# A Mixture-of-Experts kernel on one core: when SyncE asks for the weights of the next experts, and in which order

## What is computed

```python
dispatch = dispatch.at[flat_e, pos_c].add(tokens[tidx] * valid[:, None])   # 64 experts x 256 slots
g = jnp.einsum('ech,ehi->eci', dispatch, gate_w)      # gate_w, up_w: 64 x 512 x 256
u = jnp.einsum('ech,ehi->eci', dispatch, up_w)
expert_out = jnp.einsum('eci,eih->ech', jax.nn.silu(g) * u, down_w)   # down_w: 64 x 256 x 512
gathered = expert_out[flat_e, pos_c]
contrib = gathered * (topk_w.reshape(-1) * valid)[:, None]
output = jnp.zeros((t, h), tokens.dtype).at[tidx].add(contrib)
```

## Time and profile before

| | us |
|---|---|
| median of three runs | 1291.22 |
| their range | 1290.9 to 1291.5 |
| the profiled execution, as timed | 1295.88 |
| its span, first to last instruction | 1294.1 |
| PE busy | 1269.8 (98%) |
| DVE busy | 930.5 (72%) |
| ACT busy | 648.2 (50%) |
| POOL busy | 421.5 (33%) |
| HBM read and written | 178.18 MB and 71.39 MB |

### The profile page before, as it was taken

The page is one execution under the profiler, slowest core; times in us unless marked ns, Lnnn a source line. Parts: engine busy times, 40 slices in busy tenths (PEclk is TensorE's granted clock), DMA queues, the critical chain, the costliest instruction groups (busy, mean ns, idle before and its releaser), DMA issues.

```text
span 1294.1 us, 23005 instructions
## 1 busy us (share of the span) xinstructions
PE 1269.8 (98%) x7577; PEld 1118.6 (86%) x7577; DVE 930.5 (72%) x1853; ACT 648.2 (50%) x1130; POOL 421.5 (33%) x344
## 2 busy tenths in 40 slices
PE   8999999999999999999999999999999999999993
PEld 7888888888888888888889999999999999999993
DVE  7887787867878678785655777777777777777771
ACT  6422223222232223322255777777777777777771
POOL 1000000000000000000013666666666667677753
PEclk9999999999999999999999999999999999999997
DMA  8246654575545755446447999999999999999995
GB/s 309 85 137 153 135 132 113 143 168 115 133 111 145 168 107 137 112 116 136 137 132 211 297 288 302 290 299 293 298 289 297 293 293 284 299 290 301 286 250 66
DMA packets 204777, 263.66 MB, mean 204 GB/s; under 512 B 41012, under 2 KB 131016, under 8 KB 204744
## 3 DMA queue, kind: packets, MB, share of 16 engines
q1 hardware_dynamic: 175272, 191.40, 51.5%
q0 software_dynamic: 28672, 71.32, 24.5%
q10 hardware_dynamic: 800, 0.53, 0.2%
HBM read 178.18 MB, written 71.39 MB: 193 GB/s over the span
## 4 chain that ended last, share of the span: by engine, by line
PE 91%; POOL 3%; issue 3%; DVE 1%; DMA 1%; ACT 0%; POOLq 0%; ACTq 0%
PE pmm L1344 17%; PE pmm L1343 17%; PE pmm L1342 16%; PE pout L1342 11%; PE pout L1344 11%; PE pout L1343 11%; PE ptr L1599 4%; PE plp L1407 2%; POOL out_dram L1758 2%; POOL xbuf L1748 1%; PE pmm L1617 1%; PE ptr L1354 1%; DMA out_dram<-xbuf,slot_cols 1%; PE plp L1436 1%; PE plp L1416 1%
## 5 line engine op out<-in xcount | busy, mean ns | idle before, releaser
L1344 PE MATMUL pmm<-xt_hi,proj_lo 128*128 128x256 f32 (+1 forms) x768 | 241.2, 314 | 0.0
L1343 PE MATMUL pmm<-xt_lo,proj_hi 128*128 128x256 f32 (+1 forms) x768 | 241.1, 314 | 0.0
L1344 PE MATMUL pmm<-xt_hi,sgu_lo 128*128 128x256 f32 (+1 forms) x764 | 240.1, 314 | 0.0
L1343 PE MATMUL pmm<-xt_lo,sgu_hi 128*128 128x256 f32 (+1 forms) x764 | 240.1, 314 | 0.0
L1342 PE MATMUL pmm<-xt_hi,proj_hi 128*128 128x256 f32 (+1 forms) x736 | 232.5, 316 | 0.0
L1342 PE MATMUL pmm<-xt_hi,sgu_hi 128*128 128x256 f32 (+1 forms) x732 | 231.3, 316 | 0.0
L1742 POOL TENSOR_TENSOR earlier<-earlier,chosen 128x64 bf16<-128x64 bf16 x64 | 24.2, 378 | 611.4 <-DVE chosen L976 607.7
L1748 POOL DMA_INDIRECT xbuf<-rows,slot_cols x128 | 165.6, 1294 | 85.7 <-issue 37.4
L569 ACT ACTIVATE feat<-pmm,ab 128x512 f32<-128x512 f32 x66 | 45.4, 689 | 286.4 <-PE pmm L1344 286.4
L1343 PEld LDWEIGHTS pmm<-xt_lo,proj_hi 128*128 128x128 f32 x768 | 144.2, 188 | 11.2
L1343 PEld LDWEIGHTS pmm<-xt_lo,sgu_hi 128*128 128x128 f32 x764 | 143.4, 188 | 11.2
(11 more groups left out here) (220 smaller groups left out, 2640.1 us busy)
## 6 DMA issues: line engine op xcount, KB each, us to landing
raw<-in_L_ffn_gate_w_dram SPq DMA_DIRECT2D x64, 512.0 KB
raw<-in_L_ffn_up_w_dram SPq DMA_DIRECT2D x64, 512.0 KB
raw<-in_L_ffn_down_w_dram SPq DMA_DIRECT2D x64, 512.0 KB
outs<-in_L_attn_x_dram SPq DMA_DIRECT2D x32, 512.0 KB, 3.7
out_dram<-outs SPq DMA_DIRECT2D x32, 512.0 KB, 3.1
xbuf<-in_L_attn_x_dram SPq DMA_DIRECT2D x52, 256.0 KB, 8.1
raw<-xn SPq DMA_DIRECT2D x52, 256.0 KB, 6.5
rows<-raw SPq DMA_DIRECT2D x39, 256.0 KB, 4.8
```

The costliest lines, as they stand in the source:

```text
L1343: pe.matmul(psum, lh, rl, start=False, stop=False)
L1344: ins = pe.matmul(psum, ll, rh, start=False, stop=final and n == len(pairs) - 1)
```

## The change

Only SyncE's stream in the experts' part changes. Its unit becomes `refill(n)`: wait until `e_turned` says that TensorE has turned the rows of expert n-2, request gate of n, request down of n-2, request up of n. Each request keeps the wait on its own buffer. Gate and up of expert 3 stay outside, as do the two downs at the end. The first pass of the loop is written out, since expert 4 to 7's waits need constants.

```diff
-            def refill_gate_up(e):
-
-                for m, source in enumerate((gate_w, up_w)):
-                    sp.wait_ge(egu_hi_made[m], e.n - 1)
-                    sp.wait_ge(egu_lo_made[m], e.n - 1)
-                    load_half(e.b, m, source[e.n])
+            def refill_half(e, m, source):
+
+                sp.wait_ge(egu_hi_made[m], e.n - 1)
+                sp.wait_ge(egu_lo_made[m], e.n - 1)
+                load_half(e.b, m, source[e.n])
...
-            refill_gate_up(turn(3))
-            refill_down(turn(2))
-            with sp.Fori(0, CHUNKS - 3) as m:
+            def refill(e):
+
+                sp.wait_ge(e_turned, 2 * (e.n - 1))
+                refill_half(e, 0, gate_w)
+                refill_down(e.prev().prev())
+                refill_half(e, 1, up_w)
+
+            refill_half(turn(3), 0, gate_w)
+            refill_half(turn(3), 1, up_w)
+            for k in range(CHUNK):
+                refill(turn(CHUNK + k))
+                if k == 1:
+                    load_chunk(3)
+            with sp.Fori(1, CHUNKS - 3) as m:
                 for k in range(CHUNK):
-                    e = Turn(2 * m + 2 + k // 2, k % 2, k // 2)
-                    refill_gate_up(e)
-                    refill_down(e.prev())
+                    refill(Turn(2 * m + 2 + k // 2, k % 2, k // 2))
                     if k == 1:
                         load_chunk(m + 3)
             for n in range(E - 2 * CHUNK, E):
-                refill_gate_up(turn(n))
-                refill_down(turn(n - 1))
+                refill(turn(n))
+            refill_down(turn(E - 2))
             refill_down(turn(E - 1))
```

## The result

The changed kernel takes 1305.42 us, the median of 19 runs (1293.12 to 1310.42), against 1291.22 us of the kernel before on the same chip (19 runs, 1290.49 to 1295.70). The ratio is 1.010, with a 95% interval of 1.0082 to 1.0118. It is slower, and above the top of the predicted range. Its profiled execution was timed at 1304.72 us, its span is 1303.0 us.

A forecast was written before the change was run, and what follows sets the result against it. TensorE and the DMA engines were taken as full, with GpSimd's adds setting the end. Late weights cost 0 and the adds' mean cycle changes by 0, so 1291.0 us was predicted, range 1285 to 1299 us.

The forecast's parts named there:

- What bounds the kernel: Experts' part: TensorE and DMA engines both full; TensorE sets the chain to 1207.20 us, then GpSimd's adds to 1286.99.
- The wait and gate's 0.76 us; down; up: SyncE's requests: gate 0.76 us later, down 0.37 us behind it, up unchanged, then 6.4 us without a request.
- Weights in time: Experts' weights: landing bounds 3.7 and 9.8 us; even at 9.8, 2.6 us or more remain before use; cost 0.
- rival E: Experts' weights: down lands too late, 0.2 us for 60 experts, 12 us, giving 1303 us; chance 0.06.
- a bunch of two matrices delays an add by up to one more: DMA engines: if everything queued first goes first, gate and down together delay an add by up to one more matrix.
- I take 0 for the mean and let the resting place of the lag decide: GpSimd's adds: mean cycle change 0, bounded by 2.1 us either way; where GpSimd's lag behind ScalarE's copies rests decides.
- Held firmly at the last: GpSimd's lag: leaves its 3.2 us place as early or earlier, then stays at about 9.7 us, second add in the gap.
- rival A: End of the experts: GpSimd's lag again ends at 9 to 10 us, TensorE's time unchanged, 1291 us; chance 0.36.
- rival D: GpSimd's gathers land late, TensorE waits from a lag of about 10 us; 7.5 us slower, 1299 us; chance 0.23.
- The carry-over from the profile to the median: Whole kernel: median 4.66 us below the profiled 1295.88, so only differences carried; expert 59's first add moves the end equally.
- one step of 3.3: GpSimd's lag rises in steps of about 3.3 us; one step less at the end gives 1287.9 us, chance 0.24.

The follow-up runs named there:

- the halved adds: Second add of each expert left out: from the changed kernel 1284.80 us, ratio 0.9944; from the kernel before 1284.85 us, ratio 0.9934.
- order alone: Changed kernel without SyncE's wait on e_turned, keeping the new request order: 1290.11 us, ratio 0.998; again on another chip 1290.14 us, ratio 0.998.
- wait alone: Kernel before plus the wait on e_turned ahead of gate, request order unchanged: 1289.52 us, ratio 0.9984; again 1289.93 us, ratio 0.9978.
- wait alone, pushed: Kernel before plus the e_turned wait, and GpSimd once holding expert 16's adds until expert 17's first output: 1306.33 us, ratio 1.0081.
- order alone, pushed: Changed kernel without the e_turned wait, and GpSimd once holding expert 16's adds until expert 17's first output: 1308.39 us, ratio 1.0112.

## Why the prediction was wrong

- **What bounds the kernel** held: TensorE and GpSimd's adds. The adds were the right place to look, as the halved adds show.
- **The wait and gate's 0.76 us; down; up** held: 0.18 us behind the transposes, down 0.54 us behind gate (forecast 0.4), 6.4 us without a request.
- **Weights in time** (0 us, rival E at 0.06) held. Landings are 5.7, 7.2 and 7.7 us, between the bounds of 3.7 and 9.8, and no ScalarE copy waited for them. That a burst costs an add nothing in the mean was my estimate; order alone agrees, at 1290.1 us and with the second add landing 6.3 us after its issue over experts 30 to 56, against 6.9 in the wait alone, whose requests are spread and whose lag is 3.2. From 841 to 842 us of the changed kernel, with up of 838.22 and the add of 839.95 both on their way, the packets of SyncE's queue take 90.7% of the sixteen engines' time and those of GpSimd's 15.9%. In what order one engine takes them, and so whether a bunch of two matrices delays an add by up to one more, no run here shows.
- **"I take 0 for the mean and let the resting place of the lag decide".** The 0 held: over experts 30 to 56 the cycle of the adds is 9.43 us in the profile before and 9.46 in the one after. "Held firmly at the last" held too, at 8.1 to 11.2 us from expert 25 on. The step that failed is what this last place costs: rival A's "TensorE's time is unchanged" at a lag of 9 to 10 us, taken because the kernel before had ended there. The runs showed in its place that the late place leaves the gathers 1.0 us in hand instead of 6.4, that 10 of 27 are late, and that TensorE waits for them from expert 30 on, 8.8 us by expert 63. The profile before was no evidence that the place is free. It showed just seven experts near it, 57 to 63 at 8.8 to 10.3 us, and since the gather of n goes out before the adds of n-4, only the gathers of 62 and 63 came after it. The one of 63 landed 0.1 us before its transposes. Its row, 3.8 us from issue to transposes, was read for rival D and should have been put against A, because A and D are the same lag with and without a reserve. A second thing was missed: the new order has an earlier and better place, at 0.5 us; the analysis looked only at the places that the profile before showed.
- **Rival D** (0.23, slower) was the mechanism: gathers late, TensorE waits. In detail it was off. It was to decide from a lag of about 10 us, and its sign was a lag over 10 before expert 50; gathers were late from 8.1 us on, and up to expert 50 the lag was never over 9.8. Its longer cycle was there only in the slide, 10.0 us over experts 15 to 24. Its price was mis-sized, 0.15 us for 50 experts, 7.5 us: measured, the change runs at 9.46 us an expert against 9.24 over experts 30 to 56, so 0.22 us, and loses more over the last seven, 8.9 us in all between the profiles.
- **The carry-over from the profile to the median** failed as well. The profiled execution of before was 4.66 us above the median, and I carried only differences. The difference of medians, 14.20 us, is 8.84 us between the profiled executions, 0.70 us from there to the median of after, and 4.66 us of before's profile over its own median. That 4.66 us is probably a matter of lag at the end: order alone, with 4.1 us at expert 63 for 10.3, has a span of 1287.7, 6.4 us below 1294.1, and 4.66 us lie between one step of 3.3 and two. No trace shows the kernel before at its median. If this is so, A that "ends where it did" meant a kernel at 1296, not at 1291.
- **What turns the early place into the late one** is understood in kind only. In the order alone (lag 0.5) the second add of a pair lands 6.4 us after its issue, counted from the landing events over experts 2 to 14. In the change at the same lag it is 6.8 us; gate and down are asked for 0.7 us later, and up lands some 0.6 to 1.0 us later, over the adds. During the slide it is 7.45 us and a cycle 10.0. In both kernels both adds are issued while nothing is asked for, but the second lands some 3.5 us after the next gate request, so neither has its data moved in the gap alone. Why a wait 0.4 us earlier or 1.6 us later is less harmful than the one on all eight transposes, 6 and 4 good runs of 10 against none of 29, is open. Chips were not the same for all of these runs.

Of the kernels tried, the wait with the order of before is the steadiest: 20 of 22 runs within 1288.75 to 1291.66, on two chips where the kernel before had medians of 1291.72 and 1294.84; ratios 0.9984 and 0.9978, each with an interval that ends at 1.0. A gain of 0.2% is suggested and not shown.

## What to carry to other kernels

Where an engine off the critical path runs in a loop with transfers whose duration depends on when they are issued (here 6.4 to 7.45 us for the second add), ask for its resting places and for what the worst of them leaves to those who depend on it; a mean cost per step doesn't see this. A one-time delay of that engine is a cheap probe: if the kernel doesn't come back (here 7.79 us of waiting, once, cost the order alone 18 us), its good time holds only as long as nothing disturbs it, and runs in clumps are the sign to look for. A profile that lies above the median of its kernel, here by 4.66 us, may show another place than most runs, so settle that before carrying a difference over.

## What the runs showed of the hardware

GpSimd's rows for gathers and adds are their issue and not the transfer: in the order alone the second add of expert 34 is a row of 1.57 us, and it lands 6.2 us after the row's start. Nor is this work constant. The indirect issues (page, part 5: count, busy us, mean ns of one), in the order alone and in the change:

```profile
L1755 POOL DMA_INDIRECT xbuf<-rows,slot_cols x128 | 164.1, 1282 | 198.8 <-DVE slot_w L1268 155.6
```

```profile
L1756 POOL DMA_INDIRECT xbuf<-rows,slot_cols x128 | 181.1, 1415 | 111.1 <-DVE slot_w L1269 54.3
```

The same issue of 128 token rows takes 133 ns more in the mean, 1.06 us or 2.04 us in single cases, and between these two runs the size goes with the place: for experts 35 to 61 the first gather takes 1.09 us in the order alone, and 1.88 to 2.05 us in the change. In the wait alone, pushed, it takes 1.39 us in the mean, at a lag of 10.7. Over experts 30 to 56 the four issues of an expert take 6.0 us in the order alone, 7.1 in the change and 7.2 in the order alone, pushed. So a longer issue is a second thing, beside longer landings, by which the late place may keep itself up; no run here separates the two. What makes an issue short or long, no run here shows.

DMA engines that show 9 in every slice, and a share of 1.02 to 1.05 in the windows, don't tell whether anyone waits for them: between 880 and 1240 us the kernels with late gathers show 1.01 to 1.04 and 282 to 288 GB/s, those without, with full adds, show 1.03 to 1.05 and 292 to 295.
